# Scaling the attention probabilities on GpSimd: four per-partition scalings per step, or one product with the broadcast reciprocal sums

## The chip, the cores and the metric

The kernel runs on one core of a Trainium2 chip. The metric is the device time of one execution in microseconds. The core has TensorE (PE in the profile, its weight loads apart as PEld), VectorE (DVE), ScalarE (ACT), GpSimd (POOL) and SyncE (SP), which work side by side and wait for each other on semaphores.

## The reference

The input is `x`, (4, 1024, 256) in fp32. What is computed is `x + attention(xn) + moe(xn)` with `xn = layernorm(x)`.

```
qkv = xn @ w_qkv                      # 16 heads of 16 columns
# blocks of 64 tokens; a query block sees its own block and the one before it
scores = where(band_mask, q @ k.T / sqrt(16), -1e30)      # 64 x 128 for each block and head
attn   = softmax(scores, axis=-1)
out    = (attn @ v, heads side by side) @ w_out
```

The mixture of experts has 8 experts, 2 for each token, a capacity of 1,024 tokens for each expert, a 256 to 1024 to 256 network with relu, and fp32 weights. The change touches only the last part of the softmax: the division of the exponentials by their sum.

## The kernel before

Four phases run one after the other: layer norm (`norm_phase`), routing (`route_phase`), the experts (`moe_phase`) and the attention (`attention_phase`, about 495 us to the end of the span). The attention is cut into 8 units of 512 tokens; `body` runs a batch of two units, and the two middle batches are one loop on every engine.

A unit has 16 steps (`STEPS`), and so there are 128 steps in all. A step handles two heads of four blocks (`BLK = 4`), which is a tile of 128 rows by 4 x 128 columns of scores. The order of the work is written out by hand in each engine's `steps` or `body`, with fixed lags between the stages. For a step t:

- TensorE computes scores into PSUM (`scores`, L1172).
- VectorE reads each block's scores, adds the mask, keeps the row's smallest negated value and writes `a_p` in SBUF (L1051, four instructions, inputs one PSUM tile and the mask in SBUF).
- ScalarE takes the exponential in place and sums each row (L1021, four instructions).
- VectorE takes the reciprocals of the four sums of each row in one instruction (L1058, `rsum`); it does so in its step t+1, right behind the four instructions on the next scores.
- GpSimd scales `a_p` in place by `rsum` (L952, four instructions). It waits for `rsum_done` first.
- TensorE transposes the four blocks into PSUM in its step t+3 (L1186), after a wait on `norm_done`, a count that GpSimd raises. VectorE copies the result to SBUF in its step t+4 (L1065), and TensorE multiplies by the values every fourth step (L1206).

`a_p` has `PR = 8` slots, so a slot is written again eight steps later.

Each VectorE step is, in this order: four instructions on scores, the reciprocals (L1058), the copy of transposed probabilities (L1065), and then what is due in that step. What is due comes from a plan (`done_at`, made by costs and shares per step) and from lags. For step s of a unit: the low part of the transposed inputs in s=1 (L1032, twice); the copies of the keys in s=5 and s=8 (L1036, from SBUF to SBUF, and L1038); the addition of a row of the output product in s=9 to 12 (L1104, one input in PSUM); the addition of a gathered expert row into `a_res` in every odd s (L1084, `yg` and `res` both in SBUF); the second half of the group output in s=1, 5, 9, 13 (L1092, one input in PSUM); and its low part in s=2, 6, 10, 14 (L1097, both inputs in SBUF).

GpSimd's queue is, for every step, the wait and the scalings, and in even steps one gather of expert rows by an indirect DMA (L962) behind them; once in a unit also a small copy of indices (L967). `alone` is a helper that splits a wait from the instruction behind it.

Elsewhere GpSimd runs products or differences of two tensors too: L362 and L615 (fp32, both inputs in SBUF) and L369 (bf16, whose second input is broadcast along the innermost dimension).

Of the kernel before, what the change touches and what calls it, by code (L numbers as in the profile page):

```python
# [15 lines left out]
ALU = mybir.AluOpType  # L16
# [3 lines left out]
P = 128  # L20
# [20 lines left out]
def alone(eng, sem, value):  # L41


    eng.wait_ge(sem, value)
    eng.sem_inc(Mem.passed, 1)
# [710 lines left out]
def attention_phase(nc, m, x, xn_dram, y_dram, out):  # L756
# [10 lines left out]
    BLK = 4  # L767
# [27 lines left out]
    with ctx:  # L795
# [12 lines left out]
        pr = sb("a_p", [P, PR, BLK, P], fp32)  # L808
        nmax = sb("a_nmax", [P, PR, BLK], fp32)
        sums = sb("a_sums", [P, PR, BLK], fp32)  # L810
        rsum = sb("a_rsum", [P, PR, BLK], fp32)
# [17 lines left out]
        max_done, exp_done, rsum_done, norm_done = (sem(f"a_{n}") for n in ("max", "exp", "rsum", "norm"))  # L829
# [11 lines left out]
        BS, HB = 2 * STEPS, NI  # L841

        def count(b, u, i, first, last):

            n = NI * u + PRO - UT + i
            if first and u == 0 and i < O_FIRST:
                n += UT
            if last and u == 1:
                n -= O_FIRST
            return b * HB + n // 2  # L850

        def there(t, i, first, last):

            u, (kind, j) = t // STEPS, ITEMS[i]
            if kind == "o" and first and u == 0 or kind != "o" and last and u == 1:
                return None
            return u, kind, j
# [7 lines left out]
        def batches(eng, body, tail):  # L865

            body(0, True, False)
            with eng.Fori(1, B - 1) as b:
                body(b, False, False)
            body(B - 1, False, True)  # L870
            tail(B - 1)

        def lagged(t, lag, first):

            return None if first and t < lag else t - lag
# [62 lines left out]
        @block.gpsimd  # L938
        def _(pool):
            slots = m.slots[:, :].rearrange("p (k t) -> p k t", k=K)  # L940
            pool.tensor_copy(idx[0][:, :, :], slots[:, :, 0:UT]).then_inc(idx_done, 1)

            for r in range(len(m.y_out)):
                pool.wait_ge(m.y_out[r], 16 * (E * ST // len(m.y_out) + 1))

            def body(b, first, last):
                for t in range(BS):
                    u, s, r = t // STEPS, t % STEPS, t % PR
                    alone(pool, rsum_done, b * BS + t + 1)
                    for j in range(BLK):  # L950
                        e = pr[:, r, j, :]
                        pool.tensor_scalar(e, e, rsum[:, r, j:j + 1], 0.0, ALU.mult, ALU.add).then_inc(norm_done, 1)  # L952
                    if s == 0:

                        alone(pool, idx_done, b * 2 + u + 1)
                    if s % 2 == 0:
                        i = s // 2

                        if not (first and u == 0 and i < YG):

                            alone(pool, acc, (b * 2 + u) * K * UT + i - YG + 1)
                        pool.indirect_dma_start(yg[i % YG][:, :], None, y_dram,  # L962
                                                bass.IndirectOffsetOnAxis(ap=idx[u][:, i % K, i // K:i // K + 1],
                                                                          axis=0)).then_inc(yg_in[i % YG], 16)
                    if s == STEPS // 2 and not (last and u == 1):

                        pool.tensor_copy(idx[1 - u][:, :, :],  # L967
                                         slots[:, :, bass.ds(b * 2 * UT + (u + 1) * UT, UT)]).then_inc(idx_done, 1)
            batches(pool, body, lambda b: None)

        @block.scalar
# [142 lines left out]
        def _(pe):  # L1114
# [40 lines left out]
            def scores(b, t, first):  # L1155

                u, s = t // STEPS % 2, t % STEPS
                if s == 0:

                    for i in (O_FIRST - 2, O_FIRST - 1):  # L1160
                        pe.wait_ge(item_free[i % 2], i // 2 + 1 if first and t == 0 else
                                   count(b, t // STEPS - 1, i, first, False) + 1)
                if not (first and t == 0):

                    pe.wait_ge(max_done, (b * BS + t - 1) * BLK)
                mt, half = s // (2 * GRP), s // GRP % 2
                for j in range(BLK):
                    blk = half * BLK + j
                    for i in range(2):
                        c = (s + i) % GRP  # L1170
                        rows = slice(32 * c, 32 * c + 32)
                        ins = pe.matmul(psS[bank_of[(t + i) % 4]][:, j * P:(j + 1) * P],  # L1172
                                        qz[u][rows, mt, blk, :, :].rearrange("p s t -> p (s t)"),
                                        kT[u][rows, mt, blk * WIN:blk * WIN + 2 * WIN], start=True, stop=True)
                        if j == BLK - 1:
                            ins.then_inc(s_done, 1)

            def steps(b, ts, first, last):
                for t in ts:
                    g = lagged(t, LAG_T, first)  # L1180
                    if g is not None and g < BS:
                        pe.wait_ge(norm_done, (b * BS + g + 1) * BLK)
                        if not (first and g < 2):
                            pe.wait_ge(pT_done[g % 2], b * STEPS + g // 2)
                        for j in range(BLK):
                            ins = pe.transpose(psP[g % 2][:, j * P:(j + 1) * P], pr[:, g % PR, j, :], m.eye[:, :])  # L1186
                        ins.then_inc(t_done[g % 2], 1)
                    g = lagged(t, LAG_V, first)
                    if g is not None and g < BS and g % GRP == GRP - 1:

                        s, n = g % STEPS, b * (BS // GRP) + g // GRP
                        mt, half = s // (2 * GRP), s // GRP % 2
                        if s == GRP - 1:

                            pe.wait_ge(shift_in, 48 * (b * 2 + g // STEPS + 1))
                        for i in (0, 1):
                            pe.wait_ge(pT_done[i], b * STEPS + g // 2 + 1)
                        if not (first and g < GRP):

                            pe.wait_ge(o_free, n)  # L1200
                        for j in range(BLK):
                            blk = half * BLK + j
                            v = (va if blk % 2 else vs)[g // STEPS % 2]
                            for c in range(GRP):
                                heads = slice(mt * P + 32 * c, mt * P + 32 * (c + 1))
                                ins = pe.matmul(psO[32 * c:32 * (c + 1), j * P:(j + 1) * P],  # L1206
                                                v[:, blk // 2, heads], pT[:, (g - GRP + 1 + c) % PTR, j, :],
                                                start=True, stop=True)
                        ins.then_inc(pv_done, 1)
                    if t < BS:  # L1210
                        for i in range(NI):
                            parts = [part for item, part in parts_at[t % STEPS] if item == i]
                            if parts and there(t, i, first, last):
                                u, kind, j = there(t, i, first, last)
                                product(kind, j, 1 - u, count(b, u, i, first, last), i % 2,
                                        16 * (b * 2 + u + 2), (b * 2 + u) * (STEPS // GRP), parts)
                    if t % 2 == 0 and (t < BS - 2 or t == BS - 2 and not last):
                        scores(b, t + 2, first)
# [3 lines left out]
            def tail(b):  # L1222
                steps(b, range(BS, BS + LAG_V + 1), False, True)
                for j in range(UT):
                    product("o", j, 1, count(b, 1, NI - UT + j, False, True), j % 2, 0, B * (BS // GRP), range(3 * KD))
            batches(pe, lambda b, first, last: steps(b, range(BS), first, last), tail)


# [62 lines left out]
```

## Time and profile before

| | us |
|---|---|
| three runs | 800.29, 804.64, 807.0 (median 804.64) |
| the profiled execution | 808.55 |
| its span | 806.8 |

| engine | busy us | share of the span |
|---|---|---|
| TensorE | 707.6 | 88% |
| TensorE weight load | 606.9 | 75% |
| VectorE | 527.1 | 65% |
| ScalarE | 479.2 | 59% |
| GpSimd | 423.1 | 52% |

The shares are means over phases with different limits. In the last 12 or so of the page's 40 slices, which are the attention, four engines are busy at the same time; there each must be read by stretches. TensorE's busy time is modelled in part, so a TensorE that reads as full may have some room. The granted clock stands beside each stretch, as a share of full speed.

### The profile page before, as it was taken

How to read it: one execution, taken by the hardware profiler on the slowest of the kernel's cores; microseconds unless marked ns; L12 is line 12 of the kernel's file. 1: busy time of each engine (PE TensorE's matmuls, PEld its weight loads, DVE VectorE, ACT ScalarE, POOL GpSimd, SP SyncE). 2: the span in 40 equal slices, each digit the busy share in tenths (PEclk: the TensorE clock that was granted, in tenths of full speed). 3: DMA queues.
4: the chain of work that ended last, by engine and by line, in shares of the span. 5: the costliest groups of instructions: out<-in, count | busy, mean ns of one | idle time of the engine just before them, and what ended most of it. 6: DMA issues, size and time to landing. Idle time of an engine off the chain costs nothing. (4 is left out here: it accounts for less than half of the span.)

```text
span 806.8 us, 18921 instructions
## 1 busy us (share of the span) xinstructions
PE 707.6 (88%) x5805; PEld 606.9 (75%) x5805; DVE 527.1 (65%) x1888; ACT 479.2 (59%) x1503; POOL 423.1 (52%) x714
## 2 busy tenths in 40 slices
PE   2643399999999999999999998999999799999976
PEld 2333279889798897979889797778787678778765
DVE  7699244453644526454453633889999879999994
ACT  2442075380834717355371733888999788998881
POOL 2555651340603315042340303889999879999992
PEclk9966589999999999999999997899999989999895
DMA  8460421231413214131231003021323223230311
GB/s 283 136 234 0 141 83 55 90 99 46 145 43 130 64 52 144 38 127 63 84 104 46 7 27 112 28 80 60 110 82 87 92 66 93 75 113 28 113 58 37
DMA packets 50941, 70.12 MB, mean 87 GB/s; under 512 B 4784, under 2 KB 43440, under 8 KB 50864
## 3 DMA queue, kind: packets, MB, share of 16 engines
q1 hardware_dynamic: 44368, 52.37, 20.0%
q0 software_dynamic: 6144, 16.79, 6.9%
q8 instruction: 35, 0.57, 0.3%
q14 instruction: 42, 0.34, 0.1%
q10 hardware_dynamic: 352, 0.04, 0.0%
HBM read 48.28 MB, written 16.78 MB: 81 GB/s over the span
## 5 line engine op out<-in xcount | busy, mean ns | idle before, releaser
L1021 ACT ACTIVATE a_p<-a_p,a_nmax 128x128 f32<-128x128 f32 x512 | 198.3, 392 | 34.3 <-DVE a_nmax L1051 33.4
L952 POOL TENSOR_SCALAR a_p<-a_p,a_rsum 128x128 f32<-128x128 f32 x512 | 199.0, 405 | 23.9 <-DVE a_rsum L1058 21.5
L692 DVE TENSOR_TENSOR m_hl<-m_hf,m_hh 128x512 fp32r<-128x512 f32 x128 | 114.7, 908 | 98.6 <-ACT m_hh L649 83.8
L55 PE MATMUL m_psY<-m_w2h,m_hh 128*128 128x256 f32 x512 | 145.0, 283 | 0.0
L55 PE MATMUL m_psY<-m_w2l,m_hh 128*128 128x256 f32 x512 | 143.9, 281 | 0.0
L55 PE MATMUL m_psY<-m_w2h,m_hl 128*128 128x256 f32 x512 | 143.8, 281 | 0.0
L645 ACT ACTIVATE m_hf<-m_psF,b1T 128x512 f32<-128x512 f32 x128 | 88.3, 690 | 88.0 <-PE m_psF L55 64.9
L1051 DVE CUSTOM_DVE_ANT_0 a_p<-a_psS,mask 128x128 f32<-128x128 f32 x512 | 116.5, 280 | 10.3 <-PE a_psS L1172 5.3
L55 PE MATMUL m_psF<-m_xh,w1h 128*128 128x512 f32 x256 | 103.5, 404 | 12.5 <-DVE m_hl L692 11.0
L613 POOL CAST m_w2h<-raw 128x2048 fp32r<-128x2048 f32 x8 | 15.2, 1898 | 185.6 <-PE m_psY L55 185.5
L55 PE MATMUL m_psF<-m_xl,w1h 128*128 128x512 f32 x256 | 101.6, 397 | 0.0
L55 PE MATMUL m_psF<-m_xh,w1l 128*128 128x512 f32 x256 | 101.6, 397 | 0.0
L1021 ACT ACTIVATION_READ_ACCUMULATOR a_p<-a_p,a_nmax 128x1 f32 x512 | 97.7, 191 | 0.0
L55 PEld LDWEIGHTS m_psY<-m_w2h,m_hh 128*128 128x128 f32 x512 | 96.5, 188 | 0.4
L55 PEld LDWEIGHTS m_psY<-m_w2l,m_hh 128*128 128x128 f32 x512 | 96.5, 188 | 0.4
L55 PEld LDWEIGHTS m_psY<-m_w2h,m_hl 128*128 128x128 f32 x512 | 96.5, 189 | 0.0
L678 DVE TENSOR_TENSOR y<-m_psY,b2b 128x256 f32<-128x256 f32 x64 | 27.1, 424 | 105.7 <-PE m_psY L55 105.7
L1186 PE MATMUL a_psP<-eye,a_p 128*128 128x128 f32 x512 | 84.3, 292 | 12.0 <-DVE a_pT L1065 6.0
L649 ACT ACTIVATE m_hh<-m_psF,b1T 128x512 fp32r<-128x512 f32 x128 | 87.6, 684 | 0.0
L1065 DVE COPY a_pT<-a_psP 128x512 f32<-128x512 f32 x128 | 84.3, 658 | 0.1
L633 ACT ACTIVATE m_xh<-m_psT 128x512 fp32r<-128x512 f32 x32 | 19.2, 598 | 106.5 <-PE m_psT L714 106.5
L1186 PEld LDWEIGHTS a_psP<-eye,a_p 128*128 128x128 f32 x512 | 58.7, 147 | 28.8 <-POOL a_p L952 12.8
(188 smaller groups left out, 1392.9 us busy)
## 6 DMA issues: line engine op xcount, KB each, us to landing
raw<-in_L_ffn_w SPq DMA_DIRECT2D x16, 1024.0 KB, 5.2
y_scratch<-y SPq DMA_DIRECT2D x64, 128.0 KB, 1.7
n_xin<-in_L_attn_x SPq DMA_DIRECT2D x8, 512.0 KB, 7.7
xn_scratch<-n_xn SPq DMA_DIRECT2D x8, 512.0 KB, 2.9
xnr<-xn_scratch SPq DMA_DIRECT2D x8, 512.0 KB, 3.9
a_res<-in_L_attn_x SPq DMA_DIRECT2D x8, 512.0 KB, 3.5
out<-a_res SPq DMA_DIRECT2D x8, 512.0 KB
b2b<-in_L_ffn_b SPq DMA_DIRECT2D x8, 128.0 KB, 7.0
```

The lines of the kernel that those rows point to most:

```text
L55: last = pe.matmul(out, a, b, start=(n_start and i == 0), stop=(n_stop and i == n - 1))
L613: pool.tensor_copy(w2h[:, :, :], raw2[:, :, :]).then_inc(w2h_done, 1)
L633: act.activation(xh[:, g % KD, (g // KD) * HALF:(g // KD + 1) * HALF], psT[g % 2][:, :], ACT.Copy)\
L645: act.activation(hf[:, u % FR, :], psF[u % 4][:, :], ACT.Relu, bias=bias)
L649: act.activation(hh[:, u // HC, u % HC, :], psF[u % 4][:, :], ACT.Relu, bias=bias)\
L678: dve.tensor_tensor(yb[:, s % YR:s % YR + 1, :], psY[s % 2][:, 0:D].unsqueeze(1), m.b2b[:, bass.ds(e, 1), :], ALU.add).then_inc(yb_done, 1)
L692: dve.tensor_tensor(hl[:, u // HC, u % HC, :], hf[:, u % FR, :], hh[:, u // HC, u % HC, :].bitcast(fp32), ALU.subtract).then_inc(hl_done, 1)
L952: pool.tensor_scalar(e, e, rsum[:, r, j:j + 1], 0.0, ALU.mult, ALU.add).then_inc(norm_done, 1)
L1021: act.activation(e, e, ACT.Exp, scale=-1.0, bias=nmax[:, r, j:j + 1], accum_out=sums[:, r, j:j + 1]).then_inc(exp_done, 1)
L1051: dve.tensor_tensor_reduce(out=pr[:, r, j, :], in0=psS[bank_of[t % 4]][:, j * P:(j + 1) * P], in1=m.mask[:, band, :], scale=-(DH ** -0.5), ...
L1065: dve.tensor_copy(pT[:, g % PTR, :, :].rearrange("p c q -> p (c q)"), psP[g % 2][:, :])\
L1186: ins = pe.transpose(psP[g % 2][:, j * P:(j + 1) * P], pr[:, g % PR, j, :], m.eye[:, :])
```

## The change

GpSimd scales all four blocks of a step with one instruction, a product of `a_p[r]` (128 x 4 x 128) with `rsum[r]` (128 x 4) broadcast along the innermost dimension. The count on `norm_done` rises by one for each step instead of four, and TensorE's wait in front of its transposes is adapted. Nothing else is touched: the order on every engine, the lags, the buffers and the DMAs stay.

```diff
                 for t in range(BS):
                     u, s, r = t // STEPS, t % STEPS, t % PR
                     alone(pool, rsum_done, b * BS + t + 1)
-                    for j in range(BLK):
-                        e = pr[:, r, j, :]
-                        pool.tensor_scalar(e, e, rsum[:, r, j:j + 1], 0.0, ALU.mult, ALU.add).then_inc(norm_done, 1)
+                    pool.tensor_tensor(pr[:, r, :, :], pr[:, r, :, :],
+                                       rsum[:, r, :].unsqueeze(2).broadcast_to([P, BLK, P]), ALU.mult)\
+                        .then_inc(norm_done, 1)
...
                     if g is not None and g < BS:
-                        pe.wait_ge(norm_done, (b * BS + g + 1) * BLK)
+                        pe.wait_ge(norm_done, b * BS + g + 1)
```

## Rows read from the trace of the kernel before

**Rows 1.** Busy us in stretches: PE, PEld, DVE, ACT, POOL; then granted clock, DMA.

```profile
495.00:531.00 36.00, 33.68 (x294) 27.05 (x292) 27.89 (x168) 29.20 (x133) 28.18 (x64) 0.76 0.22 71
...
603.00:639.00 36.00, 34.86 (x404) 28.91 (x403) 35.01 (x188) 32.93 (x149) 33.38 (x75) 1.00 0.31 94
639.00:675.00 36.00, 30.65 (x333) 24.45 (x335) 28.60 (x150) 26.89 (x118) 26.73 (x60) 0.91 0.24 65
```

**Rows 2.** Waits in the stretch 603 to 639: total us, times, longest.

```profile
PEld a_psP L1186 <- POOL a_p L952: 0.8, 2, 0.5
```

**Rows 3.** Timeline of GpSimd: start, us, what; x is the count merged.

```profile
612.60 1.71 POOL L952 TENSOR_SCALAR a_p<-a_p,a_rsum 128x128 f32<-128x128 f32 x4 [0.19 <-DVE a_rsum L1058]
614.46 0.99 POOL L962 DMA_INDIRECT a_yg<-y_scratch,a_idx  x1 [0.15 <-DVE a_rsum L1058]
```

**Rows 4.** Timeline of VectorE: step 3 of a unit, then parts of step 9.

```profile
612.23 0.17 DVE L1058 RECIPROCAL a_rsum<-a_sums 128x4 f32<-128x4 f32 x1
612.32 0.65 DVE L1065 COPY a_pT<-a_psP 128x512 f32<-128x512 f32 x1
612.90 0.47 DVE L1084 SCALAR_TENSOR_TENSOR a_res<-a_yg,gates,a_res 128x256 f32<-128x256 f32 x1
...
614.13 0.17 DVE L1058 RECIPROCAL a_rsum<-a_sums 128x4 f32<-128x4 f32 x1
...
625.36 0.17 DVE L1058 RECIPROCAL a_rsum<-a_sums 128x4 f32<-128x4 f32 x1
...
626.36 0.48 DVE L1084 SCALAR_TENSOR_TENSOR a_res<-a_yg,gates,a_res 128x256 f32<-128x256 f32 x1
```

**Rows 5.** Instructions of four lines: ns min/median/max, first and last start.

```profile
L952 POOL TENSOR_SCALAR a_p<-a_p,a_rsum x512: 362/371/682, 498.0 to 791.0; 128x128 f32<-128x128 f32 x171
L1084 DVE SCALAR_TENSOR_TENSOR a_res<-a_yg,gates,a_res x64: 467/480/709, 509.6 to 793.1; 128x256 f32<-128x256 f32 x64
L1097 DVE TENSOR_TENSOR a_oTl<-a_o,a_oTh x32: 406/412/648, 519.9 to 796.8; 128x256 fp32r<-128x256 f32 x32
L1036 DVE COPY a_k<-k x8: 182/196/587, 508.9 to 737.9; 128x64 f32<-128x64 f32 x8
```

**Rows 6.** GpSimd's two-tensor instruction on 2,048 columns, all eight.

```profile
L615 POOL TENSOR_TENSOR m_w2l<-raw,m_w2h x8: 4567/4593/4596, 103.5 to 446.9; 128x2048 fp32r<-128x2048 f32 x8
```

**Rows 7.** Timeline of VectorE and GpSimd in the routing phase.

```profile
46.75 0.42 DVE L467 TENSOR_TENSOR r_t<-r_t,r_iota_e 128x256 f32<-128x256 f32 x1
47.10 3.43 POOL L362 TENSOR_TENSOR wqkv_l<-raw_qkv,wqkv_h 128x1536 fp32r<-128x1536 f32 x1 [5.59 <-ACT wqkv_h L379]
47.66 3.32 DVE L470 TENSOR_TENSOR r_OH<-r_iota_e,r_red 128x256 f32<-128x256 f32 x1
50.49 1.50 POOL L362 TENSOR_TENSOR wout_l<-raw_out,wout_h 128x512 fp32r<-128x512 f32 x1
```

**Rows 8.** The same, around GpSimd's product with a broadcast input.

```profile
66.90 1.23 DVE L514 TENSOR_TENSOR r_ohA<-r_iota_b,r_af 128x1024 bf16<-128x1024 bf16 x1
68.04 2.28 DVE L516 TENSOR_TENSOR r_ohB<-r_iota_b,r_bf 128x2048 bf16<-128x2048 bf16 x1
68.20 3.88 POOL L369 TENSOR_TENSOR r_ohV<-r_ohA,r_iota_t 128x1024 bf16<-128x1024 bf16 x1 [11.52 <-DVE r_ohA L514]
70.24 2.92 DVE L514 TENSOR_TENSOR r_ohA<-r_iota_b,r_af 128x1024 bf16<-128x1024 bf16 x1
```

**Rows 9.** VectorE's busy us in L1084 in one stretch, with its eight instructions.

```profile
603.00:639.00 36.00, 4.04 (x8) 1.00 0.31 94
```

**Rows 10.** TensorE in two stretches: length, busy (instructions), granted clock, DMA.

```profile
500.00:510.00 10.00, 10.00 (x60) 0.68 0.10 28
510.00:520.00 10.00, 8.74 (x105) 1.00 0.09 28
```

**Rows 11.** VectorE's scores instructions two steps apart at that lower clock.

```profile
503.61 0.29 DVE L1051 CUSTOM_DVE_ANT_0 a_p<-a_psS,mask 128x128 f32<-128x128 f32 x1 [1.94 <-PE a_psS L1172]
510.00 0.28 DVE L1051 CUSTOM_DVE_ANT_0 a_p<-a_psS,mask 128x128 f32<-128x128 f32 x1
```

## The prediction

> **What bounds the kernel now.** I began with the busy time by stretches, since the shares of the whole span mix phases. The attention is a repeating unit of 16 steps, and a unit takes 36 us: in the stretch 603 to 639 VectorE is busy 35.01 of them, TensorE 34.86 at full clock, GpSimd 33.38, ScalarE 32.93 [rows 1]. VectorE has 1 us to spare in 36. TensorE's ends are modelled, so its figure is an upper bound. I take VectorE as the bound and the others as close behind. Then the waits: TensorE's weight loads wait for GpSimd's scaled tile for only 0.8 us in that unit [rows 2]. So a faster GpSimd alone can give back little. That turned the question from "how long is the new instruction" to "what does it do to VectorE", and for that I read the timelines of both engines side by side.
>
> **GpSimd's own time.** Removed are 4 x 128 scalings with a median of 371 ns [rows 5]; four of them take 1.5 us if nothing holds them and 1.71 us in a step shown [rows 3]. Added are 128 products of 512 columns. No row shows an fp32 product with a broadcast input. The plain two-tensor form takes 4.59 us for 2,048 columns in all eight cases [rows 6], and 3.43 us for 1,536 [rows 7]; per 512 columns that is 1.15 and 1.14 us. The broadcast form in bf16 took 3.88 us for 1,024 columns, but VectorE's instruction that began 0.16 us before it ended at 68.04 + 2.28 = 70.32, and 72.08 - 70.32 = 1.76 us is left for 1,024 columns [rows 8], or 0.88 us for 512. Taken at its face it would be 1.94 us. I take 1.15 us, from the rows of the right type, with 0.88 and 1.94 us as ends. GpSimd's scaling of a step thus falls by about 0.4 us, and ends 0.4 us earlier. That gain meets no wait worth more than 0.8 us in a unit.
>
> The Trainium skill (GPSIMD Engine Reference, Engine selection) speaks against the change: one-input work on GpSimd runs at about line rate and two-input work about twice as slow as on VectorE. By its rule the four scalings would need about 4 x 0.11 us of streaming, an estimate from the page's clock, and the product would be the longer one. The trace contradicts it for 128 columns (371 ns each [rows 5]), and the measurement decides: here the product is the shorter of the two.
>
> **What it does to VectorE.** Three rows show that a VectorE instruction with two SBUF inputs does not proceed while GpSimd runs a two-tensor instruction. L467 (256 columns) takes 0.42 us with GpSimd idle at its start; L470, of the same size, began 0.56 us into GpSimd's 3.43 us, and ended at 50.98, 0.45 us behind GpSimd's end at 50.53 [rows 7]. L514 took 1.23 us alone and 2.92 us beside the broadcast product, ending 1.08 us behind its end [rows 8]; so a broadcast input frees nothing. It works the other way too: the next GpSimd instruction, 512 columns, took 1.50 us instead of 1.15, about the 0.45 us by which L470 still ran [rows 7].
>
> Now the scalings. L1084 began at 612.90, in the midst of four of them, and took its minimum of 0.47 us; GpSimd's four took 1.71 instead of 1.5 us [rows 3, 4, 5]. Short scalings let VectorE in. Its median is 480 ns against a minimum of 467, the maximum 709 [rows 5].
>
> The Trainium skill (SBUF — State Buffer, Who interferes with whom) says that the two share a pair of ports under an exclusive lock, held for the whole instruction. The long instructions agree with it (the 3.32 us of L470); the scalings agree less, since by the rule L1084 would have waited there for the rest of a scaling.
>
> **How much is held, step by step.** A free GpSimd starts 0.37 us after the start of the reciprocals (612.60 against 612.23) [rows 3, 4]. A product of 1.15 us then ends at 1.52 us. VectorE's own next instructions: the copy from PSUM, untouched, and at 0.67 us (612.90) whatever is due. If it has two SBUF inputs, or is the key copy from SBUF to SBUF, it is held for 1.52 - 0.67 = 0.85 us. Behind an output row (L1104, one PSUM input, not held) it starts at 1.00 us (626.36 - 625.36) [rows 4] and is held 0.52 us. By the plan of a unit:
> - L1084: s = 3, 7, 13, 15 at 0.85 us, s = 9, 11 at 0.52 us; s = 1 comes after two long instructions and s = 5 after a held key copy, so nothing.
> - L1097: s = 2, 6, 14 at 0.85 us, s = 10 at 0.52 us.
> - L1036: s = 5, 8 at 0.85 us. That it can be held shows in 587 against 182 ns [rows 5].
>
> That is 9 x 0.85 + 3 x 0.52 = 9.2 us in a unit. GpSimd must not be late for this. In an odd step it ends the product at 1.52, then needs 0.16 us and the gather's 0.99 us [rows 3], so it is free at 2.67 us; the next reciprocals come at 1.90 us (614.13 - 612.23) plus the hold of 0.85, at 2.75 us. It is in time for each one, so the collision repeats.
>
> To subtract: what VectorE loses already, 4.04 - 8 x 0.467 = 0.3 us in L1084 [rows 9, 5] and about 0.3 us in the two key copies (between 0 and 2 x 0.4 us [rows 5]); and of its 1 us idle, half, because the wait for the inputs' high part stays in front of L1032. Net 9.2 - 0.6 - 0.5 = 8.1 us in a unit. VectorE is the bound, so this goes to the end of the span; the 0.4 us that GpSimd saves gives nothing then, as its result is wanted only two steps later.
>
> **The sum.** Six of the eight units look like that of 603 to 639: 6 x 8.1 = 48.6 us. The unit from 639 to 675 has VectorE busy for 28.60 us, with its gaps in one place where all engines stand, so I count 7 us. The first has 27.89 us [rows 1] with scattered gaps that can swallow holds: I choose half, 4 us. The last batch has no key copies in its second unit: -1.7 us. Sum +57.9 us. The profiled execution took 808.55 us, so 866.5 us; the median of the runs is 3.9 us lower: **862 us**. What costs nothing: TensorE's changed count (it waited for all four scalings before too), and the fewer semaphore increments.
>
> The likeliest case's own range: with 0.88 us for the product the holds are 0.58 and 0.25 us, 6.0 us gross and 4.9 net, scaled to +35 us, 840. With the stall and first unit counted in full and a product of 1.25 us, +70 us, 875. So 838 to 880.
>
> **The rivals.**
> 1. *VectorE is let in, and the time falls or stays.* If the product reads in short pieces as the scalings do, no hold grows, and GpSimd's 0.4 us lets TensorE go earlier. Price: at most the 1 us of VectorE's idle time in each of 8 units [rows 1], 808.55 - 8, on the median 797; with no gain 804. For it: L1084's minimum of 0.47 us inside scalings [rows 4]. Against it: L514 beside a broadcast product [rows 8]. It decides if the hold of each of the 12 instructions stays under 0.08 us.
> 2. *TensorE's clock falls.* VectorE's holds leave TensorE about 34.9 of 44 us busy, 79%. In the first unit the granted clock was 0.68 over ten us, so in part the lower level of 1.2 GHz, and two steps took 6.4 us there (503.61 to 510.00), TensorE busy throughout; yet 1.00 at 8.74 of 10 us busy [rows 10, 11]. Two steps are forecast at 5.5 us, so each pair at that clock adds 0.9 us, 54 us if all 60 did; I take two fifths, +22 us, 884.
> 3. *The product is slow*: 3.88 us at its face, 1.94 us for 512 columns. It ends at 2.31 us; the holds are 1.64 and 1.31 us, 18.7 us gross, 17.6 net, and 57.9 x 17.6 / 8.1 = +126 us, 930. Against it: the remainder of 1.76 us fits VectorE's end exactly.
>
> **How the numbers follow.** Forecast 0.66, the first rival 0.14 (0.08 faster, 0.06 the same), the second 0.15, the third 0.05. I leave out the first rival and the third, and reach halfway from the forecast's lower end towards no loss, for holds swallowed by slack elsewhere: 825 to 908. Differences under 1% are not told from none here. Faster 0.08, same 0.06, slower 0.86.
>
> **What would show it.** The product at 1.1 to 1.2 us; L1084 with a mean near 1.1 us, L1097 near 1.2 us, while L1092 and L1104 keep 0.47 and 0.40 us; GpSimd idle before L952 in nearly every step, released by the reciprocals; VectorE still busy near 97% of a unit of 44 us. It is wrong if L1084 keeps 0.48 us, and its size is wrong if units lengthen by less than the holds add up to.

## The result and the profile after

The changed kernel takes 835.67 us (median of four, 835.48 to 836.89) against 805.82 us for the kernel before in the same comparison: a ratio of 1.039, 95% interval 1.0347 to 1.0434. It is slower by 29.9 us. The forecast was slower, 862 us in a range of 825 to 908; the mechanism came as described and the size was about half. The 835.67 us lie just below the 838 to 880 us that the forecast gave its own likeliest case; they are inside the wider range only. Its profiled span is 835.1 us, 28.3 us more than before.

The page of the changed kernel, engine by engine and then two of its groups (busy us, mean ns of one, then idle time before them and what ended it; L950 is the product):

```profile
PE 715.0 (86%) x5804; PEld 608.6 (73%) x5805; DVE 568.9 (68%) x1888; ACT 481.9 (58%) x1503; POOL 358.1 (43%) x330
...
L950 POOL TENSOR_TENSOR a_p<-a_p,a_rsum 128x512 f32<-128x512 f32 x128 | 133.3, 1041 | 118.0 <-DVE a_rsum L1058 118.0
```

GpSimd lost 65 us of work and gained idle time: it waits for the reciprocals in front of nearly every product. VectorE gained 41.8 us of busy time with the same 1,888 instructions. So something that VectorE already did has become longer. The busy time by stretches, which answers to [rows 1], with the same columns:

```profile
495.00:531.00 36.00, 31.07 (x276) 24.82 (x274) 31.15 (x160) 28.62 (x129) 21.80 (x22) 0.81 0.23 70
...
603.00:639.00 36.00, 32.84 (x374) 26.44 (x374) 36.00 (x167) 29.68 (x132) 22.84 (x23) 1.00 0.29 86
```

VectorE is busy for 36.00 of 36 us, and gets 167 instructions done where it did 188. TensorE (32.84 us) and ScalarE (29.68 us) have room, at a granted clock of 1.00. Which instructions grew, min/median/max in ns as in [rows 5]:

```profile
L950 POOL TENSOR_TENSOR a_p<-a_p,a_rsum x128: 1038/1041/1055, 497.5 to 818.3; 128x512 f32<-128x512 f32 x128
L1084 DVE SCALAR_TENSOR_TENSOR a_res<-a_yg,gates,a_res x64: 467/998/1036, 508.8 to 822.3; 128x256 f32<-128x256 f32 x64
L1097 DVE TENSOR_TENSOR a_oTl<-a_o,a_oTh x32: 415/1000/1009, 520.2 to 825.1; 128x256 fp32r<-128x256 f32 x32
L1036 DVE COPY a_k<-k x8: 757/770/780, 507.5 to 761.3; 128x64 f32<-128x64 f32 x8
L1092 DVE SCALAR_TENSOR_TENSOR a_o<-a_psO,parity,a_o x32: 467/471/485, 518.3 to 824.1; 128x256 f32<-128x256 f32 x32
L1104 DVE TENSOR_TENSOR a_res<-a_res,a_psA x32: 399/405/422, 557.7 to 831.2; 128x256 f32<-128x256 f32 x32
```

L1084 and L1097, with both inputs in SBUF, went from 480 and 412 to about 1,000 ns, the key copy L1036 from 196 to 770. L1092 and L1104, which read one input from PSUM, did not move. The timeline of VectorE in three steps, and then that of GpSimd (start, us, what), shows how:

```profile
564.86 0.65 DVE L1065 COPY a_pT<-a_psP 128x512 f32<-128x512 f32 x1
565.43 0.41 DVE L1104 TENSOR_TENSOR a_res<-a_res,a_psA 128x256 f32<-128x256 f32 x1
...
566.60 0.17 DVE L1058 RECIPROCAL a_rsum<-a_sums 128x4 f32<-128x4 f32 x1
566.69 0.65 DVE L1065 COPY a_pT<-a_psP 128x512 f32<-128x512 f32 x1
567.27 1.00 DVE L1084 SCALAR_TENSOR_TENSOR a_res<-a_yg,gates,a_res 128x256 f32<-128x256 f32 x1
568.19 0.47 DVE L1092 SCALAR_TENSOR_TENSOR a_o<-a_psO,parity,a_o 128x256 f32<-128x256 f32 x1
...
597.91 0.67 DVE L1084 SCALAR_TENSOR_TENSOR a_res<-a_yg,gates,a_res 128x256 f32<-128x256 f32 x1
```

```profile
565.12 1.04 POOL L950 TENSOR_TENSOR a_p<-a_p,a_rsum 128x512 f32<-128x512 f32 x1 [0.23 <-DVE a_rsum L1058]
566.95 1.04 POOL L950 TENSOR_TENSOR a_p<-a_p,a_rsum 128x512 f32<-128x512 f32 x1 [0.79 <-DVE a_rsum L1058]
568.13 1.00 POOL L962 DMA_INDIRECT a_yg<-y_scratch,a_idx  x1
...
597.26 1.04 POOL L950 TENSOR_TENSOR a_p<-a_p,a_rsum 128x512 f32<-128x512 f32 x1 [1.76 <-DVE a_rsum L1058]
```

The product starts at 566.95, 0.35 us behind the reciprocals, and ends at 567.99. L1084 starts in its midst and ends at 568.27, 0.28 us behind the product's end. Behind an output row it has 0.67 us (597.91), ending at 598.58 against 598.30: the same 0.28 us. L1104, from 565.43 to 565.84, passes beside the product of 565.12 untouched.

### The profile page after: what moved, and what is told of

The parts are those of the page before. It is cut to its first block and busy times, and to the rows that moved or that the text cites. A ratio compares the mean times of both kernels' runs of the same rounds, so it can differ in the third digit from the quotient of the medians.

```text
span 835.1 us, 18534 instructions
## 1 busy us (share of the span) xinstructions
PE 715.0 (86%) x5804; PEld 608.6 (73%) x5805; DVE 568.9 (68%) x1888; ACT 481.9 (58%) x1503; POOL 358.1 (43%) x330
## 5 line engine op out<-in xcount | busy, mean ns | idle before, releaser
L950 POOL TENSOR_TENSOR a_p<-a_p,a_rsum 128x512 f32<-128x512 f32 x128 | 133.3, 1041 | 118.0 <-DVE a_rsum L1058 118.0
L692 DVE TENSOR_TENSOR m_hl<-m_hf,m_hh 128x512 fp32r<-128x512 f32 x128 | 116.4, 922 | 89.6 <-ACT m_hh L649 89.5
L1186 PE MATMUL a_psP<-eye,a_p 128*128 128x128 f32 x512 | 86.9, 299 | 25.7 <-DVE a_pT L1065 22.7
L1065 DVE COPY a_pT<-a_psP 128x512 f32<-128x512 f32 x128 | 83.7, 655 | 0.0
```

Source lines behind the costliest of these rows:

```text
L692: dve.tensor_tensor(hl[:, u // HC, u % HC, :], hf[:, u % FR, :], hh[:, u // HC, u % HC, :].bitcast(fp32), ALU.subtract).then_inc(hl_done, 1)
L950: pool.tensor_tensor(pr[:, r, :, :], pr[:, r, :, :], rsum[:, r, :].unsqueeze(2).broadcast_to([P, BLK, P]), ALU.mult)\
L1065: dve.tensor_copy(pT[:, g % PTR, :, :].rearrange("p c q -> p (c q)"), psP[g % 2][:, :])\
```

## The experiments

All changes are to the changed kernel unless it says otherwise. The ratios are to the kernel before, run on the same chip in the same comparison. Its own median was 805.82, 809.5, 803.64 and 807.65 us in the four comparisons, so runs of different comparisons are best set against each other by their ratios. The lines of VectorE's instructions shift by a few in these kernels; the text keeps the numbers of the kernel before. A hold is time by which a VectorE instruction is longer than alone, because GpSimd runs beside it.

### Length or kind of GpSimd's instruction

**Four products of 128 columns.**

```diff
-                    pool.tensor_tensor(pr[:, r, :, :], pr[:, r, :, :],
-                                       rsum[:, r, :].unsqueeze(2).broadcast_to([P, BLK, P]), ALU.mult)\
-                        .then_inc(norm_done, 1)
+                    for j in range(BLK):
+                        pool.tensor_tensor(pr[:, r, j:j + 1, :], pr[:, r, j:j + 1, :],
+                                           rsum[:, r, j:j + 1].unsqueeze(2).broadcast_to([P, 1, P]), ALU.mult)\
+                            .then_inc(norm_done, 1)
...
-                        pe.wait_ge(norm_done, b * BS + g + 1)
+                        pe.wait_ge(norm_done, (b * BS + g + 1) * BLK)
```

> GpSimd scales a step by four products of 128 columns, each with its broadcast reciprocal sum, where the changed kernel has one of 512; all else as in the changed kernel. My theory: VectorE's instructions with two SBUF inputs are held until the GpSimd instruction under way has nearly ended, so the hold follows the length of one instruction, not the kind. A product of 128 columns should take about 0.3 us; L1084 should fall from a median of 998 ns to 480 to 620 ns, VectorE's gaps return, and the time come to 800 to 812 us. Rival 1: any two-tensor instruction of GpSimd keeps the ports, back to back, so that VectorE gets in only behind the fourth: L1084 stays near 1,000 ns or more and the time at 833 to 840 us. Rival 2: the loss came from something else in the change (one count for each step, where it starts): also 833 to 840 us, but with L1084 at 480 ns.

Measured: 819.3 us, 1.0114 (1.0082 to 1.0146), between the 800 to 812 us of my theory and the 833 to 840 us of its rivals. A product of 128 columns takes 398 ns. L1084 (here L1085) has a median of 477 ns but a mean of 702 and a maximum of 1,690, and the pattern repeats in each unit. The timelines of this kernel, first GpSimd's, then three instructions of VectorE:

```profile
568.57 0.99 POOL L963 DMA_INDIRECT a_yg<-y_scratch,a_idx  x1 [0.16 <-issue]
569.58 2.89 POOL L951 TENSOR_TENSOR a_p<-a_p,a_rsum 128x128 f32<-128x128 f32 x8
...
588.78 3.60 POOL L951 TENSOR_TENSOR a_p<-a_p,a_rsum 128x128 f32<-128x128 f32 x8 [1.04 <-DVE a_rsum L1059]
...
593.54 3.25 POOL L951 TENSOR_TENSOR a_p<-a_p,a_rsum 128x128 f32<-128x128 f32 x8
```

```profile
571.11 1.65 DVE L1085 SCALAR_TENSOR_TENSOR a_res<-a_yg,gates,a_res 128x256 f32<-128x256 f32 x1
...
590.94 0.47 DVE L1085 SCALAR_TENSOR_TENSOR a_res<-a_yg,gates,a_res 128x256 f32<-128x256 f32 x1
...
595.70 0.48 DVE L1085 SCALAR_TENSOR_TENSOR a_res<-a_yg,gates,a_res 128x256 f32<-128x256 f32 x1
```

Eight products in a row, the work of two steps, end at 572.47, and L1084 ends at 572.76, 0.29 us later. It was let in behind none of those that ended in between. The hold can be longer than one instruction when GpSimd has a row of ready ones. At 590.94 it is otherwise: L1084 ends at 591.41, 0.97 us before the row of 588.78 does, and that row takes 3.60 instead of 2.89 us. Rival 1 is right in places of the first sort and my theory in those of the second.

**Two products of 256 columns**, written the same way with `j in (0, 2)`; TensorE's wait counts two for each step.

> The changed kernel with the step's product cut in two of 256 columns, issued back to back. From 398 ns for 128 columns and 1,041 ns for 512 I expect about 0.6 us each. Theory A, drawn from the run with four products, where an L1084 that met eight products in a row was held for 1.65 us to the end of the row: back-to-back products do not let VectorE in between, so the pair holds like one of 1.2 us; L1084's median is 1.05 to 1.2 us and the time 836 to 846 us. Theory B: VectorE gets in between any two instructions; L1084's median is 0.5 to 0.8 us and the time 812 to 826 us.

Measured: 823.19 us (817.67 to 827.21), 1.0221 (1.0147 to 1.0294). L1084's median is 572 ns. The time and the median are those of theory B, but each theory is right in some places, as two places in GpSimd's timeline and the two instructions of VectorE that met them show:

```profile
570.96 1.19 POOL L951 TENSOR_TENSOR a_p<-a_p,a_rsum 128x256 f32<-128x256 f32 x2
573.55 1.37 POOL L951 TENSOR_TENSOR a_p<-a_p,a_rsum 128x256 f32<-128x256 f32 x2 [1.40 <-DVE a_rsum L1059]
```

```profile
571.16 1.28 DVE L1098 TENSOR_TENSOR a_oTl<-a_o,a_oTh 128x256 fp32r<-128x256 f32 x1
573.88 0.57 DVE L1085 SCALAR_TENSOR_TENSOR a_res<-a_yg,gates,a_res 128x256 f32<-128x256 f32 x1
```

At 573.88 VectorE is let in behind the first product, and the pair takes 1.37 instead of 1.19 us. At 571.16, with a pair that followed straight on a gather, it is held to the end of both (572.15, and 0.29 us more). In these two places of this trace, and in those shown of the one before, the row that keeps VectorE out had not waited for the reciprocals just before. That alone does not decide: the row of 593.54 above had not waited either, and let L1084 in at 595.70 (0.48 us). What decides was not separated.

**One scaling of 512 columns**, with one factor.

```diff
-                    ...                                  # the product
+                    e = pr[:, r, :, :]
+                    pool.tensor_scalar(e, e, rsum[:, r, 0:1], 0.0, ALU.mult, ALU.add).then_inc(norm_done, 1)
```

> GpSimd scales the 512 columns of a step by one tensor_scalar with the first block's reciprocal sums; the right factors of the other three blocks are left out. One SBUF tensor input, one instruction. My theory (length decides): if it takes 0.6 to 1.5 us, L1084 behind the copy is held to about 0.2 us short of its end, so L1084's median is 0.60 us at a length of 0.6 us and up to 1.45 us at a length of 1.5 us, and the time 808 to 860 us accordingly. Rival (the second input decides, since only it loads the shared read side twice): L1084 keeps a median of about 480 ns whatever the length, and the time is 797 to 808 us.

Measured: 814.42 us, 1.0057 (1.0036 to 1.0078). It takes 0.70 us, and L1084's median is 666 ns, not 480: my theory, and not the rival. The trace of this kernel at one hold (L1096 is L1097 of before):

```profile
575.79 0.70 POOL L951 TENSOR_SCALAR a_p<-a_p,a_rsum 128x512 f32<-128x512 f32 x1 [1.50 <-DVE a_rsum L1057]
576.08 0.67 DVE L1096 TENSOR_TENSOR a_oTl<-a_o,a_oTh 128x256 fp32r<-128x256 f32 x1
```

576.08 + 0.67 = 576.75, 0.26 us behind the scaling's end at 576.49. So a scaling with one SBUF tensor as its input holds VectorE too; the second input is not needed. That fits the kernel before as well: a scaling of 371 ns that starts 0.30 us ahead of L1084 ends 0.07 us into it, and 0.28 us more is still within L1084's own 0.47 us, so nothing shows.

### Taking the collision away

**VectorE's three instructions moved** from behind the copy of transposed probabilities to just ahead of the reciprocals.

```diff
-                    dve.tensor_copy(kT[u][:, j, 0:WIN], kT[1 - u][:, j, UL:UL + WIN])
...
+                    g = lagged(t, LAG_Y, first)
+                    ...                                  # L1084 as it was
+                    g = lagged(t, LAG_O + 1, first)
+                    ...                                  # L1097 as it was
+                    for i, u, kind, j in ended(lagged(t, LAG_I, first), first, last):
+                        if kind == "k":
+                            dve.tensor_copy(kT[(1 - u) % 2][:, j, 0:WIN], kT[1 - (1 - u) % 2][:, j, UL:UL + WIN])
                     g = lagged(t, 1, first)
                     if g is not None and g < BS:
                         dve.wait_ge(exp_done, (b * BS + g + 1) * BLK)
...
-                    g = lagged(t, LAG_Y, first)
-                    ...
-                    g = lagged(t, LAG_O + 1, first)
-                    ...
```

> The changed kernel, with VectorE's three instructions that can be held (L1084, L1097, L1036) moved within its step from behind the copy of transposed probabilities to just ahead of the reciprocals, where GpSimd has ended the product of the step before. Nothing is left out. My theory: all holds vanish (medians 470, 410 and 190 ns), and the 29 us are won back with the 0.6 us in a unit that the kernel before loses too: 796 to 806 us. Rival 1: the loss is not the holds: 825 to 836 us. Rival 2: the moved instructions stand ahead of the reciprocals and of what ScalarE must deliver (L1097 waits for it), so that a new wait takes their place: 806 to 820 us, with VectorE idle in front of L1097.

Measured: 803.25 us, 0.9923 (0.9897 to 0.9948), as the theory said. The whole loss is gone, and nothing but the order of VectorE's own instructions was changed. L1084 (here L1065) is back at a median of 485 ns, and VectorE is busy for 36.00 us of 36 with 196 instructions, where the kernel before had 34.98 and 190:

```profile
L1065 DVE SCALAR_TENSOR_TENSOR a_res<-a_yg,gates,a_res x64: 474/485/906, 506.0 to 788.4; 128x256 f32<-128x256 f32 x64
```

```profile
567.00:603.00 36.00, 35.36 (x418) 29.31 (x411) 36.00 (x196) 33.60 (x152) 25.71 (x27) 1.00 0.31 91
```

Not every hold is gone: in steps 1 and 5 L1084 still takes about 0.81 to 0.88 us.

> The same move in the kernel before, with its four scalings; a control. My theory: little to win, since the holds are 0.6 us in a unit there: 799 to 808 us. Rival 2 of the run before (the moved order itself costs): 810 to 822 us, the same addition as there.

Measured, the same order with the four scalings: 805.77 us, 0.9954 (0.9934 to 0.9975). The order costs nothing by itself and is worth a little even without the product. The two runs together hold the answer: in the old order the product costs 3.9%, and in this one it costs nothing (803.25 against 805.77 us, with intervals that overlap). So the loss was in the collisions of the product with these three instructions.

**Only L1084 moved, and only the other two moved.**

> The changed kernel with only L1084 moved ahead of the reciprocals; L1097 and L1036 stay behind the copy and stay held. If the loss is the sum of the holds: L1084 is 4 x 0.53 + 2 x 0.20 = 2.5 us of the 5.5 us in a unit, so 46% of the 32 us that moving all three won back: 818 to 824 us. Rival: one kind alone makes the loss, so 803 to 808 us or 833 to 836 us.

> The changed kernel with L1097 and L1036 moved, L1084 left behind the copy and held. If the loss is the sum of the holds, the other 54% come back: 815 to 821 us, and together with the run that moves L1084 alone the two gains add up to the 32 us. Rival as there; a second rival is that the gains don't add up, because another engine is the bound as soon as half is gone: both runs at 808 to 814 us.

Measured: 833.1 us, 1.0366 (1.0304 to 1.0428), with L1084 moved; 816.04 us, 1.0161 (1.0097 to 1.0224), with the other two. The gains are about 2.6 and 19.6 us and do not add up to 32; by the ratios they are 0.2% and 2.3% against 4.7% for all three. The second run lies in its range; the first does not, and lies where its rival had it. The trace of the kernel with L1084 moved says why. Its timelines, VectorE first (L1066 is L1084 of before):

```profile
570.42 1.32 DVE L1097 TENSOR_TENSOR a_oTl<-a_o,a_oTh 128x256 fp32r<-128x256 f32 x1
...
575.91 0.87 DVE L1066 SCALAR_TENSOR_TENSOR a_res<-a_yg,gates,a_res 128x256 f32<-128x256 f32 x1
```

```profile
569.39 0.99 POOL L962 DMA_INDIRECT a_yg<-y_scratch,a_idx  x1
570.39 1.05 POOL L950 TENSOR_TENSOR a_p<-a_p,a_rsum 128x512 f32<-128x512 f32 x1
...
575.44 1.05 POOL L950 TENSOR_TENSOR a_p<-a_p,a_rsum 128x512 f32<-128x512 f32 x1
```

VectorE's step is now shorter than GpSimd's product and gather, so GpSimd is late in these places: the next product starts at 570.39, straight behind the gather. L1097 behind the copy meets it 0.03 us after its start and takes 1.32 instead of 1.00 us. The key copy's median rose likewise, from 770 to 867 and 1,126 ns. The moved L1084 is itself held in some steps (0.87 us at 575.91). About half of what it was spared, the others paid: its time fell by 15.5 us, from 51.8 to 36.3, and VectorE's time in the three lines only by 7.6, from 91.2 to 83.6 us.

### Does a microsecond of hold cost what a microsecond of work costs?

**Delays in place of the holds**: with all three moved, a reduction of 440 constant columns behind the copy in the 12 steps of a unit that had a hold.

```diff
+        COLS = 220
...
+                    if t < BS and t % STEPS in (2, 3, 5, 6, 7, 8, 9, 10, 11, 13, 14, 15):
+                        dve.tensor_reduce(dummy[:, t % 32:t % 32 + 1], m.wout_h[:, :, 0:COLS].bitcast(fp32), AX.XY, ALU.max)
```

> The changed kernel with all three moved (no holds), and a reduction of 440 constant columns, which writes one unused column, added on VectorE behind the copy in the 12 steps of a unit in which the changed kernel has a hold. It has one SBUF input, so it should not be held; I expect 0.45 to 0.6 us of VectorE's time each. Theory: VectorE's time in these places goes to the end of the span whatever it is spent on: added time is 96 times what one takes, less up to a tenth, which is 803 + 40 to 803 + 55 us. Rival (a hold costs more or less than its length, because the ports and not VectorE's time are the matter): 803 to 825 us.

Measured: 841.35 us, 1.0481 (1.0419 to 1.0542), 2 us below the range of the theory and far from the rival's. The reduction takes 601 ns. VectorE's busy time rises by 43.7 us over the kernel without it (573.7 against 530.0) and the span by 35.1: 0.80 us for each. For the holds, the changed kernel against the moved one, it is 568.9 - 530.0 = 38.9 us and a span longer by 32.9: 0.85. Where the attention begins differs a little between these traces, though nothing ahead of it was changed: its first instruction on scores starts at 496.3 us with all three moved, at 494.2 with the delays and at 495.0 in the changed kernel. Counted from there, the two are 0.85 and 0.88. A hold costs about what the same length of honest work costs in that place. The rest went out of VectorE's idle time.

**GpSimd's scaling nearly left out** (one column of 512), in the changed kernel's order.

> GpSimd scales one column of a step only; the scaling of the other 511 is left out. VectorE's order is that of the changed kernel. A floor for what any form of GpSimd's scaling costs in that order: no holds. Theory: L1084, L1097 and L1036 at their least (467, 406, 182 ns), VectorE's excess nearly 0, and by the line 796 us; if VectorE alone set the pace it could not be lower than that. Rival: GpSimd's work costs in other ways too (its result is late for TensorE), so the floor is well below, at 785 to 791 us.

Measured: 798.84 us, 0.9894 (0.9859 to 0.993). The floor is near 799 us: all that any form of the scaling can give in this order is about 1%, and moving the three instructions had given 0.8%. VectorE is no longer full there: in the stretch 567 to 603 it is busy for 35.49 us of 36, and TensorE, close behind, for 35.30.

In one table, for one profiled execution each: VectorE's time in the three lines above its least (64 x 0.467 + 32 x 0.406 + 14 x 0.183 = 45.5 us), the span, and the attention's part of it, from the start of the first instruction on scores. The three rows with "refined" or "again" are of the section behind this one.

| kernel | above the least, us | span, us | attention, us |
|---|---|---|---|
| scaling left out | 0.8 | 796.5 | 302.3 |
| all three moved, again | 6.8 | 799.4 | 304.7 |
| all three moved | 7.5 | 802.2 | 305.9 |
| all three moved, four scalings | 7.4 | 802.2 | 307.9 |
| refined order | 6.9 | 804.5 | 309.0 |
| refined order, four scalings | 6.5 | 806.4 | 311.9 |
| before | 5.9 | 806.8 | 311.4 |
| one scaling of 512 | 17.4 | 811.8 | 317.7 |
| L1097 and L1036 moved | 22.4 | 814.8 | 319.0 |
| four products | 23.6 | 818.7 | 321.7 |
| two products | 25.0 | 825.5 | 326.5 |
| L1084 moved | 38.1 | 831.1 | 334.9 |
| changed | 45.7 | 835.1 | 340.1 |

The ends give (340.1 - 302.3) / 44.9 = 0.84 us of attention for each us. Most rows lie within 3 us of that line. The kernel before and the refined order with four scalings lie 5 us above it, and the two products 4 us. So holds are most of the story among the slow kernels and not among the fast ones: the kernel before loses less to them than the one with the same scalings and the three moved, and is longer by 3.5 us. In a stretch inside the loop (567 to 603) VectorE is busy for 34.98 us of 36 in the kernel before, for 35.50 with the three moved and four scalings, and for 36.00 with the three moved and the product. What the order gives beyond the holds seems to be this idle time; no run separates it.

### A last version

> The changed kernel with the three instructions moved ahead of the reciprocals, but L1084 left at its old place in steps 1 and 5 of a unit. In the run with all moved, L1084 took 0.81 to 0.88 us in just these steps: the step before is a short one, so the product before is still under way; at its old place it stood behind long instructions and was free. Theory: all 64 take about 0.48 us, VectorE's excess falls from 7.5 us to about 1 us, and at 0.86 us of span for each us of excess (the line through the four kernels with one product of 512) the time is 5 to 6 us under the run with all moved: 795 to 800 us, 0.984 to 0.990 of the kernel before. Rival: TensorE and ScalarE are the bound by then (their busy time is 35.4 and 33.6 of 36 us with all moved), and the time stays within 2 us of that run, 0.990 to 0.994.

> The same order of VectorE's work with the kernel before's four scalings: what the product itself is worth once the order suits it. Theory: GpSimd's 33 of 36 us stay the limit here, so the time is 800 to 805 us, 0.993 to 0.998 of the kernel before, and the kernel with the product is faster by 3 to 6 us. Rival: the scaling's form doesn't matter in this order: both within 2 us of each other.

> The kernel with all three moved, again, beside the two others so that differences under 1% can be told: 0.990 to 0.995 of the kernel before, as the first time.

```diff
-                    if g is not None and g < BS and g % 2 == 0:          # L1084, ahead of the reciprocals
+                    if g is not None and g < BS and g % 2 == 0 and t % STEPS not in (1, 5):
...
+                    if g is not None and g < BS and g % 2 == 0 and t % STEPS in (1, 5):          # behind the copy
```

Measured, in this order: 806.23 us, 0.9985 (0.9968 to 1.0002); 810.1 us, 1.0024 (1.0003 to 1.0044); and with all three moved again 802.9 us, 0.9931 (0.9907 to 0.9956). My refinement was worse than what it refined, by 3.3 us where I had expected 5 to 6 us to be won, and outside the rival's range too. With the four scalings the time missed its range of 800 to 805 us as well; the distance between product and scalings, 3.9 us, is in the 3 to 6 us expected. So in a suitable order the product is worth 0.3 to 0.5%. The groups of VectorE in the refined kernel (busy us, mean ns), the last with its idle time:

```profile
L1075 DVE COPY a_k<-k 128x64 f32<-128x64 f32 x8 | 3.1, 386 | 0.0
L1075 DVE COPY k<-a_k 128x64 f32<-128x64 f32 x6 | 2.7, 449 | 0.0
...
L1032 DVE TENSOR_TENSOR a_xTl<-a_psA,a_xTh 128x512 fp32r<-128x512 f32 x14 | 9.1, 687 | 4.3 <-ACT a_xTh L979 4.2
```

In step 5 the late product now holds the key copy (386 and 449 ns, against 214 and 219 with all moved), which stands where the held L1084 had stood; the three lines are 6.9 us above their least, not 1. In step 1 VectorE arrives at L1032 before ScalarE's part is there (4.2 us of idle time, 2.9 in the other); the held L1084 had covered part of that wait. These two do not add up to the whole difference between the two traces (309.0 against 304.7 us of attention); the rest stays open. So the best version here is the changed kernel with all three moved: 0.992 and 0.993 of the kernel before in two comparisons, 5 to 6 us.

## Why the prediction was right in its way and wrong in size

- **VectorE is the bound, and GpSimd's speed is worth little.** Right. VectorE went from 35.01 to 36.00 us of 36, and GpSimd's 65 us less of work bought nothing that shows in this order.
- **The product's length**: 1.15 us forecast from [rows 6, 7], 1.04 us measured. The row nearest in size was L362's 512 columns: 1.50 us less the 0.45 us for which it was held, 1.05 us [rows 7]. I had used that row for the holding and not for the length. The Trainium skill (GPSIMD Engine Reference, Performance versus the Vector engine) gives about 2.6 cycles for each element with two inputs, which at the page's clock is an estimate of 1.11 us; the trace is 6% lower. The inner broadcast costs nothing that shows, against those 1.05 us of a product without it.
- **Who is held, and who is not.** Right for all of L1084, L1097, L1036, L1092 and L1104, and so was the list of steps: free in steps 1 and 5, short behind an output row.
- **The length of a hold.** This is the term that was mis-sized. I took the hold as the product's end less VectorE's start, and let VectorE's whole instruction run after it: 0.85 us. Measured is 1.00 - 0.47 = 0.53 us. The difference is 0.11 us of the product's length, 0.02 us of its start, and 0.19 us because only 0.28 us of VectorE's 0.47 is left when the product ends. The rows of before had it: L514 ended 1.08 us behind the broadcast product though it takes 1.23 us alone [rows 8]. I quoted both numbers and did not subtract them. L470 had pointed the other way, ending 0.45 us behind with a length of 0.42 us alone, and I went by it. Behind an output row it is 0.20 instead of 0.52 us, and for the key copy 0.59 instead of 0.85 us.
- **The sum for a unit.** L1084 4 x 0.53 + 2 x 0.20, L1097 3 x 0.59 + 0.26, L1036 2 x 0.59: 5.7 us instead of 9.2. I subtracted 0.6 us for what was lost before, which was right (0.64), and 0.5 us of idle time, where all of the 1.0 us went, the wait in front of L1032 too (the changed kernel's rows below show none). 5.7 - 0.64 - 1.0 = 4.1 us. Measured from one L1032 to the next: 607.55 - 571.74 = 35.81 us before and 616.30 - 576.47 = 39.83 us after, 4.0 us, where I had 8.1. The rows are VectorE's timeline of the kernel before, then of the changed one:

```profile
571.74 1.29 DVE L1032 TENSOR_TENSOR a_xTl<-a_psA,a_xTh 128x512 fp32r<-128x512 f32 x2 [0.54 <-ACT a_xTh L979]
...
607.55 1.29 DVE L1032 TENSOR_TENSOR a_xTl<-a_psA,a_xTh 128x512 fp32r<-128x512 f32 x2 [0.51 <-ACT a_xTh L979]
```

```profile
576.47 1.27 DVE L1032 TENSOR_TENSOR a_xTl<-a_psA,a_xTh 128x512 fp32r<-128x512 f32 x2
...
616.30 1.27 DVE L1032 TENSOR_TENSOR a_xTl<-a_psA,a_xTh 128x512 fp32r<-128x512 f32 x2
```

- **The sum over the units.** By the starts of L1032 three more regular units grew by 4.1, 5.2 and 4.1 us, the first unit by 1.1 where I had chosen 4, and the one with the stall by 3.2 where I had 7. What follows the last L1032 took 7.1 us more. So the terms of the first and the stalled unit were too large as well. The end of the range that holds the measured time had been widened for slack elsewhere; most of what was missing was the length of a hold. That the time still fell inside owes something to luck.
- **GpSimd in time for each step, so that the collision repeats.** Right: it waits for the reciprocals 126 times out of 128. The run that moved L1084 alone shows what happens where it is late: holds get longer (1.32 instead of 1.00 us).
- **The rivals.** "VectorE is let in" is refuted by every hold. "TensorE's clock falls" did not come: the granted clock is 1.00 in the stretch shown and 0.934 over the span, as before, and TensorE is busy for 32.84 us of 36 there. "The product is slow" is refuted by 1.04 us; that the 3.88 us of [rows 8] were mostly a wait for VectorE, as the remainder suggests, fits this, but no run tested that instruction.
- **The scalings and the rule.** I wrote that the scalings agree less with the lock that the Trainium skill describes (SBUF — State Buffer, Who interferes with whom). They need not disagree: a hold to the end of one scaling of 371 ns would be hidden in what of VectorE's own length runs beside the wait, and the one long scaling did hold it to its end. What does go beyond the page's "whole instruction" is the row of eight products, which kept VectorE out across several instructions.
- **Why the product is the shorter one.** I read the 371 ns of a scaling as a contradiction to 0.11 us of streaming. The runs separate the two parts: a scaling of one column takes 267 ns, of 128 columns 371 and of 512 columns 697 ns. That is (697 - 371) / 384 = 0.85 ns for a column, 0.11 us for 128, and some 260 ns for each instruction. The product is shorter than four scalings because it has that part once, and longer than one scaling of the same 512 columns (1.04 against 0.70 us).

## What to carry to other kernels

Before making GpSimd's work into fewer, longer instructions, list VectorE's instructions with two SBUF inputs, or from SBUF to SBUF, that start while it runs: here each was held to the end of the GpSimd instruction under way, and VectorE, as the bound, paid it at nearly the full price. The cure is the order, not the form: put those instructions where GpSimd waits anyway, here just ahead of the instruction that releases it. Here moving L1084 alone gave almost nothing and a refinement made it worse, so move them together and measure each refinement: a hold that is spared in one place changes who is late and can come back on the next instruction.

## What the runs showed of the hardware that was not expected

- A VectorE instruction of 256 columns that is held ends 0.26 to 0.30 us behind the end of GpSimd's instruction in the places shown, where its own length is 0.41 to 0.47 us. Some 0.1 to 0.2 us of it runs beside the wait. The key copy of 64 columns (0.18 us alone) ends 0.06 us behind (changed kernel: 586.33 + 0.77 = 587.10, the product at 587.04).
- GpSimd's one-input scaling takes 267 ns for one column, 371 for 128 and 697 for 512; the product takes 398, 613 and 1,041 ns for 128, 256 and 512. For 512 columns the one long scaling is the shortest form, but has only one factor for each row.
- Rows of ready GpSimd products kept VectorE out for as long as 1.65 us over several instructions, while in other places it was let in while the row went on. What decides stays open.
